# A fused four-layer graph network on one core: the layer-norm statistics, the first weight cast and three mixing groups moved around the end of the edge stage

## The reference

```
edge_index = stack([src, dst])
h = max(layernorm(x), 0);  x = x + L0(h)   # normalised adjacency, 2 rounds of A @ h @ W_gcn @ W_mlp, leaky relu
h = max(layernorm(x), 0);  x = x + L1(h)   # 4 blocks: conditioned norm, sparse attention (4 heads), norm, MLP
h = max(layernorm(x), 0);  x = x + L2(h)   # 3 diffusion steps with the symmetric adjacency
h = max(layernorm(x), 0);  x = x + L3(h)   # 2 relational layers, 2 relations each
```

## Time and profile before

| | us |
|---|---|
| median of 3 runs | 873.79 (873.46 to 874.17) |
| span of the profiled execution | 871.2 |
| time of the profiled execution outside its span | not recorded; median less span is 2.6 |
| PE busy | 833.7 (96%) |
| DVE busy | 559.8 (64%) |
| ACT busy | 397.5 (46%) |
| POOL busy | 230.5 (26%) |
| mean granted TensorE clock | 0.990 of 2.4 GHz |
| DMA | 113.42 MB, mean 130 GB/s |

### The profile page before, as it was taken

The page is one execution under the profiler, slowest core; times in us unless marked ns, Lnnn a source line. Parts: engine busy times, 40 slices in busy tenths (PEclk is TensorE's granted clock), DMA queues, the critical chain, the costliest instruction groups (busy, mean ns, idle before and its releaser), DMA issues. The chain is left out here.

```text
span 871.2 us, 13200 instructions
## 1 busy us (share of the span) xinstructions
PE 833.7 (96%) x4222; PEld 633.8 (73%) x4223; DVE 559.8 (64%) x1221; ACT 397.5 (46%) x646; POOL 230.5 (26%) x253
## 2 busy tenths in 40 slices
PE   5999789999889999999999999999999999999998
PEld 3666457767577779777787787787786976688786
DVE  7999987748957675676668576764766665720210
ACT  4999893325345622355423364233663235431200
POOL 4000023208431025502226122334013424422200
PEclk9999999999999999999999999999999999999999
DMA  8989934715516653644634447436367368130100
GB/s 188 204 208 230 259 82 120 179 59 133 160 54 123 183 136 109 149 104 125 165 103 138 113 101 200 94 109 147 104 184 187 120 185 209 50 97 1 49 13 36
DMA packets 59349, 113.42 MB, mean 130 GB/s; under 512 B 4372, under 2 KB 4936, under 8 KB 59292
## 3 DMA queue, kind: packets, MB, share of 16 engines
q1 hardware_dynamic: 42108, 79.00, 38.4%
q10 hardware_dynamic: 17184, 33.69, 11.9%
HBM read 105.33 MB, written 7.34 MB: 129 GB/s over the span
## 5 line engine op out<-in xcount | busy, mean ns | idle before, releaser
L686 POOL TENSOR_TENSOR wl<-wraw,wh 128x512 fp32r<-128x512 f32 x140 | 180.2, 1321 | 386.6 <-ACT wh L764 353.2
L1802 PE MATMUL ring<-ohs,ohd 128*128 128x512 f32 x312 | 79.3, 406 | 6.6 <-DVE ohs L1313 6.5
L1802 PEld LDWEIGHTS ring<-ohs,ohd 128*128 128x128 f32 x312 | 58.8, 194 | 31.3 <-issue 18.7
L1291 DVE SCALAR_TENSOR_TENSOR ohd<-iota,dstT,vals 128x256 fp32r x156 | 69.6, 481 | 4.9 <-issue 3.4
L764 ACT ACTIVATE wh<-wraw 128x2048 fp32r<-128x2048 f32 x35 | 66.9, 1910 | 9.2 <-DMA wraw<-in_L_gnn_wk 4.8
L789 ACT ACTIVATE yT_h<-ring 128x512 fp32r<-128x512 f32 x32 | 19.0, 597 | 97.8 <-PE ring L1718 97.8
L813 ACT ACTIVATE ohs<-iota,minus_srcT 128x512 fp32r<-128x512 f32 x78 | 52.3, 713 | 13.3 <-PE ring L1802 7.0
L691 POOL TENSOR_TENSOR rstd<-ve,half 128x1 f32<-128x1 f32 x44 | 24.1, 550 | 105.8 <-DVE ve L1142 105.5
L1729 PE MATMUL mix_ps<-quad,att_shift 120*32 120x512 f32 x384 | 50.3, 603 | 1.5 <-DMA quad<-in_L_gnn_basis 1.5
L1700 PE MATMUL ring<-yT_l,wh 128*128 128x512 f32 x128 | 49.8, 389 | 0.0
L1700 PE MATMUL ring<-yT_h,wh 128*128 128x512 f32 x128 | 49.8, 389 | 0.0
(11 more groups left out here) (390 smaller groups left out, 2150.1 us busy)
## 6 DMA issues: line engine op xcount, KB each, us to landing
quad<-in_L_gnn_basis SPq DMA_DIRECT2D x60, 960.0 KB, 8.1
wraw<-in_L_gnn_m_w ACTq DMA_DIRECT2D x8, 1024.0 KB, 9.4
mix_scratch<-mixed SPq DMA_DIRECT2D x128, 32.0 KB
wraw<-in_L_gnn_wv ACTq DMA_DIRECT2D x4, 1024.0 KB, 5.2
wraw<-in_L_gnn_wq ACTq DMA_DIRECT2D x4, 1024.0 KB, 5.2
wraw<-in_L_gnn_wk ACTq DMA_DIRECT2D x4, 1024.0 KB, 5.4
wraw<-in_L_gnn_wo ACTq DMA_DIRECT2D x4, 1024.0 KB, 5.2
wraw<-mix_scratch ACTq DMA_DIRECT2D x4, 1024.0 KB, 5.6
```

What stands on the lines that cost most here:

```text
L686: last = g.tensor_tensor(wl[s][:, k, :], wraw[s][:, k, :], wh[s][:, k, :].bitcast(F32), ALU.subtract)
L1291: return v.scalar_tensor_tensor(out, at.unsqueeze(1).broadcast_to([P, 4, HALF]), dstT[:, e], vals[:, e, :].rearrange("p a b -> p (a b)").u ...
L1802: last = te.matmul(ring[:, banks[b], :], ohd[:, s, b, :], ohs[:, s, :], start=False, stop=False)
```

## The change

- DVE: the statistics of x leave the place between the sure and the later units. They come one tile at a time by `norm_stats` (L1134 to L1142), tiles 0 and 1 behind `marks_made` and before the last eviction, tiles 2 and 3 behind it.
- POOL: `root_and_mean(t)` for each tile, all four ahead of `low_weight(0)`.
- ACT: `hw(0)` comes behind the last marks and ahead of the last eviction; the xn0 rows come behind the eviction, each ahead of its transposes and interleaved with the splits. `take_set(NT)` (set 4) comes right behind `hw(1)`, `take_set(NT + 1)` (set 5) ahead of the G splits instead of behind the U splits.
- PE: the outer `If` and loop over the later units 32 to 39 are written out, with `mix_groups(1)` between k = 8 and k = 9; `mix_groups(2)` instead of 1 behind the last unit. The list `early` holds ten groups, so (6, 0) comes after G and (6, 1) after U; (6, 2) and (6, 3) stand ahead of block 0; in block 0 the mixing groups before the heads h = 1 and h = 2 are gone, the one at h = 3 and the three behind stay.
- SP: all groups, to the last set, go round the three slots of `quad`, and a load waits for the group three before it. (6, 0) and (6, 1) are loaded ahead of the counts' store; (6, 2) and (6, 3) ahead of the store of x instead of in block 0's list.

```
 def quad_place(t, k):
-    if isinstance(t, int) and t < EARLY_SETS:
-        g = t * GROUPS + k - PASS_GROUPS
-        return g % QSLOTS, (g // QSLOTS + 1) * 16
-    before = len(range(k % 2, EARLY_SETS * GROUPS - PASS_GROUPS, QSLOTS))
-    return k % 2, t * (GROUPS // 2 * 16) + (before - EARLY_SETS * GROUPS // 2 + k // 2 + 1) * 16
+    g = t * GROUPS + k - PASS_GROUPS
+    return g % QSLOTS, (g // QSLOTS + 1) * 16
...
 def load_group(t, k):
-    if not isinstance(t, int) or t >= EARLY_SETS:
-        sp.wait_ge(quad_used, t * GROUPS + (k - 1))
-    else:
-        n = t * GROUPS + k
-        sp.wait_ge(quad_used, n - (GROUPS if n < PASS_GROUPS + QSLOTS else QSLOTS) + 1)
+    n = t * GROUPS + k
+    sp.wait_ge(quad_used, n - (GROUPS if n < PASS_GROUPS + QSLOTS else QSLOTS) + 1)
...
+load_group(EARLY_SETS, 0)
+load_group(EARLY_SETS, 1)
 sp.wait_ge(ct_ready, NT)
...
-load_group(EARLY_SETS, 0)
-load_group(EARLY_SETS, 1)
 store_set(EARLY_SETS - 1)
+load_group(EARLY_SETS, 2)
+load_group(EARLY_SETS, 3)
...
 # POOL
-pool.wait_ge(ln_var, NT)
-g.tensor_tensor(rstd[:], ve[:], half[:], ALU.pow).then_inc(ln_rstd, NT)
...
+for t in range(NT):
+    root_and_mean(t, t)
 pool.wait_ge(marks_made, 1)
 low_weight(0, slot(0))
...
 # ACT
-hw(0)
 (the later units)
-act.wait_ge(ln_xn, NT)
-for t in range(NT):
-    a.activation(xn0[:, t, :], x[:, t, :], ACT.Relu, ...).then_inc(h0_hi, 1)
+hw(0)
 (the last eviction)
-for t in range(NT):
-    high(n0, n0.base, ("T", t), hb_h[0][:, :, t * P:(t + 1) * P])
+layer_rows(0); layer_rows(1); layer_turned(0); layer_rows(2)
+layer_turned(1); layer_rows(3); layer_turned(2); layer_turned(3)
 hw(1)
+take_set(NT)
...
 # DVE
-dve.wait_ge(x_loaded, 16)
-(bn_stats x 4, bn_aggr x 4, one add)
 (the later units)
 dve.drain().then_inc(marks_made, 1)
+dve.wait_ge(x_loaded, 16)
+norm_stats(x[:, 0, :], 0, 0)
+norm_stats(x[:, 1, :], 1, 1)
 (the last eviction)
+norm_stats(x[:, 2, :], 2, 2)
+norm_stats(x[:, 3, :], 3, 3)
...
 # PE
-with pe.If(count > SURE):
-    with pe.Fori(SURE // WORD, NEXT // WORD) as k:
-        later_units(k, count)
+for k in range(SURE // WORD, NEXT // WORD):
+    later_units(k, count)
+    if k == SURE // WORD:
+        mix_groups(1)
...
-mix_groups(1)
+mix_groups(2)
...
 for h in range(1, HEADS):
-    mix_in_block(1)
+    if i or h == HEADS - 1:
+        mix_in_block(1)
...
-    mix_group(EARLY_SETS, k)
+    mix_group(EARLY_SETS, GROUPS // 2 + k)
-attention_block(0, False, 2)
+attention_block(0, False, GROUPS)
```

More of the change, by code:

```diff
@@ L382, in program @@
         ln_xn = sem("ln_xn")
-        mean_step = sem("mean_step")
         h0_hi = sem("h0_hi")
@@ L576, in block_loads @@
                 t = i * BLOCK_SETS + EARLY_SETS
-                load_group(t, 2)
+                if i:
+                    load_group(t, 2)
                 load_cond(nxt, 0, i * 2 + 2)
-                load_group(t, 3)
+                if i:
+                    load_group(t, 3)
                 if not last:
@@ L872, in _ @@
                         later_units(k, count)
-            act.wait_ge(ln_xn, NT)
-            for t in range(NT):
-                a.activation(xn0[:, t, :], x[:, t, :], ACT.Relu, bias=nmean[:, t:t + 1], scale=rstd[:, t:t + 1]).then_inc(h0_hi, 1)
+            hw(0)
             with act.If(act.snap(held, min_val=0, max_val=1) > 0):
@@ L880, in _, with layer_rows, layer_turned @@
             evict(slice(NT - 1, NT), 1)
-            for t in range(NT):
+            def layer_rows(t):
+                act.wait_ge(ln_xn, t + 1)
+                a.activation(xn0[:, t, :], x[:, t, :], ACT.Relu, bias=nmean[:, t:t + 1], scale=rstd[:, t:t + 1]).then_inc(h0_hi, 1)
+            def layer_turned(t):
                 high(n0, n0.base, ("T", t), hb_h[0][:, :, t * P:(t + 1) * P])
+            layer_rows(0)
+            layer_rows(1)
+            layer_turned(0)
+            layer_rows(2)
+            layer_turned(1)
+            layer_rows(3)
+            layer_turned(2)
+            layer_turned(3)
             hw(1)
+            take_set(NT)
             act.wait_ge(emb_step, 4)
@@ L894, in _ @@
                 a.activation(An_h[:, m, :], Araw[:, m, :], ACT.Copy).then_inc(deg_act, 1)
-            take_set(NT)
             for t in range(NT):
@@ L917, in _ @@
                 a.activation(hb_h[1][:, t, :], hv[:, t % 2, :], ACT.Copy).then_inc(hi_ready, 1)
+            take_set(NT + 1)
             for m in range(KT):
@@ L927, in _ @@
             lw(5)
-            take_set(NT + 1)
             hw(4)
@@ L1732, in mix_group @@
                 ins.then_inc(quad_used, 1)
-            early = [(t, k) for t in range(NT, EARLY_SETS) for k in range(GROUPS)]
+            early = [(t, k) for t in range(NT, EARLY_SETS + 1) for k in range(GROUPS)][:10]
             def mix_groups(count):
```

## The result

The changed kernel takes **868.80 us** (median of 5 executions, 865.51 to 871.21) beside 873.79 us for the kernel before (5 executions, 872.84 to 874.78): a ratio of 0.993, interval 0.9911 to 0.995. Forecast was 871.0 us, 2.8 less. The profiled execution of the changed kernel is the fastest of its five: 865.51 us, span 864.0 us, 7.2 us under the span of before. Part of the work is therefore to tell what of the 7.2 us belongs to the change and what to that one execution.

A forecast was written before the change was run, and what follows sets the result against it. PE was taken as busy nearly all the time, following DVE's marks in the later units. Front and tail 0.2, groups 1.6, loads 1.4, small edits 0.2, clock -0.6: 2.8 us gained, 871.0 us, range 868.2 to 874.4.

The forecast's parts named there:

- part 6: PE's clock: a fall in the tail's holes may carry into V; 0.6 us lost (0 to 1.8).
- part 5: Small edits: ACT's `take_set` (0.6 us) leaves the place before `hw(4)`; 0.2 us gained (0 to 0.6).
- part 1: Front, statistics of x gone from ahead of unit 32: DVE's last mark 3.8 us sooner (2.9 to 4.5).
- part 4: Mixing group loads, three slots and earlier requests: PE's one wait for a load goes, 1.4 us gained (0 to 1.47).
- V before 128: V's start, forecast near 129.8: the forecast is wrong if it comes before 128 or after 132.
- Part 2: Tail, from DVE's last mark to V's start: grows from 6.95 to 10.5 us, 3.55 lost (2.6 to 4.7).
- Rival A: Tail in series, tiles 2 and 3 not overlapping: V 4.5 us later, time 876.7 us; chance 0.10.
- rival C: Later units: marks come no sooner than PE or ACT allow; time 872.9 us; chance 0.12.
- Part 3: Two mixing groups moved from block 0's heads into holes further ahead: 1.6 us gained (1.1 to 2.1).
- The first place: First place in block 0 losing a group: 0.5 us of 1.07 counted, the key's low part being late next.
- The second place: Second place in block 0 losing a group: no such chain of waiting shows, so 1.07 us gained in full.
- Rival E: More gain: nothing of the sequencer's 1.54 us stays, no clock fall after deg or in the tail; 867.9 us; chance 0.10.

The follow-up runs named there:

- e4: The changed kernel itself, measured again in a second comparison with the kernel before: 869.48 us, ratio 0.9933.
- e5: The changed kernel plus one wait: POOL starts the low part of block 0's first weight only when DVE has written brow; 870.22 us, ratio 0.9942.
- e1: The kernel before with the load slots alone changed: three to the end, a load waits for the group three before it; 871.74 us, ratio 0.9948.
- e10: The changed kernel with one load, group 0 of the last set, requested behind the use of the group before it; 875.19 us, ratio 1.0019.
- e6: The changed kernel with the group behind z1 moved into the middle of deg's products; 872.22 us, ratio 0.9956.
- b0: The kernel before, unchanged, measured against itself: 874.01 us, ratio 1.0006.
- b1: The kernel before, unchanged, one more execution: 873.15 us.
- e2: The kernel before with only the statistics, first cast and rows moved, groups and loads as before; 874.23 us, ratio 0.9985.
- e9: The changed kernel with every group of the later sets requested behind the use of the group before it; 875.26 us, ratio 1.001.

## Why the prediction was right or wrong

The direction and the range held; the forecast gain of 2.8 us was too small beside 5.0 by the medians and 6.1 by the ratio. The steps that failed are part 6, which charged 0.6 us for the clock and put every fall outside two windows at nothing, where the ledger shows about 1.7 us gained, and part 5, which had ACT's lighter load as a gain of 0.2 us where 1.07 were lost; part 1 was mis-sized by 1.15 us, and for part 4 medians and profiles don't agree. One of the prediction's own signs of being wrong, V before 128, came up narrowly: 127.93 in the first profile, 128.51 in e4. Term by term, by the ledger's means:

**Part 1 (3.8 forecast, 4.95 measured): mis-sized.** I left 0.7 of the 1.54 us of sequencer work standing; nothing stayed. That is 0.7 of the difference. Of the other 0.45, 0.3 is before's own spread (36.02 to 36.68), where the first profile, which I had, was the shortest. "PE has some slack in each unit and makes up most of it" holds: the group inside the units costs the last mark nothing (31.4 us in all eight profiles of kernels with this front and group).

**Part 2 (3.55 lost forecast, 3.25 measured): right,** step by step. (The same tail takes 10.2 to 10.7 us over six profiles; in the longest, e5's, PE stands 1.3 us before it closes the last half.) The hop from a tile's variance to its row is the 1.04 us of the second of rows 4 and not 1.4. PE closed 2.0 us behind the last mark (119.02 + 0.73), forecast 2.3. Front and tail together gave 1.7 us where I had 0.2. Rival A, the tail in series (V at E + 14.4), never occurred; rival C (PE or ACT lead among the marks) neither in the changed kernel.

**Part 3 (1.6 forecast, 1.2 measured): right within its bounds.** The first place gave 0.1 us by the means and at most 0.4 between any two profiles. As forecast, PE runs into the key's low part:

```profile
263.04 0.50 PE L1701 MATMUL ring<-qk_h 128*128 128x512 f32 x1 [0.95 <-DVE qk_l L1130]
```

0.95 us of waiting instead of 0.16, so 0.8 of the group's 1.07 us went into the wait. The second place gave 1.04 us, the group in full.

**Part 4 (1.4 forecast, 1.5 measured in the profiles): right in the profiles, unsettled in the medians.** The load by itself moved the medians by 3.6 us (e1). Its interval, 2.9 to 6.1 us off, leaves out 1.5. e10 shows a way for it, a wait of over 3 us that drags a fall of the clock behind it, 4.8 us; but no profile of before has it. That some of before's other executions do is argued and not shown. It matters: 3.6 is 2.2 us more than the 1.4 counted on, which by the medians would be the whole shortfall of the forecast.

**Part 5 (0.2 gained forecast, 1.07 lost): wrong, and of the wrong sign.** "DVE bounds that stretch" was true and the conclusion from it false. Taking 0.6 us of ACT's work away releases POOL 1.1 us sooner, and POOL then slows the very engine that bounds. I looked only at who waits for ACT's step, not at what it starts.

**Part 6 (0.6 lost forecast; about 1.7 gained): wrong.** Three rows of the ledger carry it. After deg: 34.5 to 34.0 us by the means, but 32.4 in one profile and 35.6 in six others. Before ln_c: 0.5 lost, since one of three profiles of before lacks the fall there (36.82 us, the 1.5 us that a fall costs where PE leads). And 1.8 gained up to the second qk_l, which I hadn't looked at: I read the clock in two windows around the change and not over the whole span, so the fall at 244 never entered the sum. With all seven profiles (35.2 us after deg) the first row turns into a loss of 0.6 and the gain of the part shrinks to 0.6. The tail's hole, the one place where I charged for the clock, cost nothing in any profile with the groups in it. The executions that were not profiled point the same way with a smaller size: mean granted clock 0.9882 for before and 0.9903 for the changed kernel in e4's comparison. Among before's own executions there, spans are 2.8 us longer at 0.984 than at 0.990 (874.5 and 871.7); by that slope 0.0021 of clock is 1.0 us.

Added up: 1.15 too little in part 1, 0.3 in part 2, 0.1 in part 4 and 2.3 in part 6 (with 0.5 the other way for the last row of 420.69, a wait for yT_l that e4 alone has), against 1.3 too much in part 5 and 0.4 in part 3. Two large errors of opposite sign left an error of 1.8 us by the ledger and 2.2 by the medians. Rival E named the conditions of the first profile exactly, nothing of the 1.54 us left and no fall after deg, and gave 867.9; its second condition held in one profile of seven.

## What to carry to other kernels

Work moved out of one hole makes another behind it: the statistics alone gave the front 4.1 us and took 4.2 from the tail; together with the groups, front and tail came out 1.7 us ahead. (Of the 1.8 us between the two kernels, 0.85 lie in front and 1.0 in the tail.) When a step leaves an engine that isn't the bound, follow what its next instruction starts, GpSimd above all, and see what DVE does at that moment: here 0.6 us less on ACT cost 1.1 us on DVE. Cutting GpSimd's long job in two around the small one that somebody waits for was worth 2 us here. And read the granted clock over the whole span and of more than one profile before crediting or charging an edit for it: the first profiled execution of the changed kernel was 3 us under its median, and e6's nearly 6 us under its own.

## What the runs showed that I had not expected

- A late load of under 1 MB costs more than its wait: 3.27 us of standing still became 4.8 us, as the half clock follows; waits of 0.95 to 1.87 us at the same place (before, b0, b1, e2) left the clock at 1.00.
- The same load takes 9.3 to 10.2 us from issue to use in the three profiles of before and 11.5 and 11.6 in e9 and e10, behind the use of the same group, with the DMA engines busy nearly throughout in all five. Why it lands later there wasn't tried.
- The collision of DVE and POOL comes in steps: four mask operations take 2.49, 3.59 or 4.72 us, 1.1 us apart. Of the latter two either can come out with POOL starting 1.17 us behind the first of them (212.04 in e4, 212.01 in e10).
- Long parts of these executions repeat to 0.1 us: the last stretch is 127.45 us in every profile of every kernel. What differs between profiles of one kernel is mostly the clock, the loads, that collision and the moment at which PE closes the last half.
